# DVE's order at a tile's end: the rest of the transposed h ahead of the second norm's statistics, the normalising operation one lo part later

## The reference, cut to what matters

```python
# N = 4096 nodes, F = 256 features, 16 experts, hidden 512
h   = layernorm(x)
Wh  = h @ W; src = Wh @ a[:F]; dst = Wh @ a[F:]
att = softmax(where(adj > 0, leaky_relu(src + dst.T, 0.2), -9e15), axis=1)   # 4096 x 4096
h_prime = att @ Wh
gi = h_prime @ w_ih.T + b_ih; gh = h @ w_hh.T + b_hh          # 3F columns each
r = sigmoid(i_r + h_r); z = sigmoid(i_z + h_z); n = tanh(i_n + r * h_n)
x  = x + (1 - z) * n + z * h
xn2 = layernorm(x)                                           # the second norm
probs = softmax(xn2 @ gate_w + gate_b); top-2, renormalised
x  = x + sum over the two experts of weight * ((silu(xn2 @ w1) * (xn2 @ w2)) @ w3)
```

## Time and profile before

| | before |
|---|---|
| runs | 1268.34, 1272.80, 1272.82 us |
| median of the runs | 1272.8 us |
| profiled execution: its own time | 1271.41 us |
| its span | 1269.7 us |
| PE busy | 1158.3 us (91%) |
| PEld busy | 1052.3 us (83%) |
| DVE busy | 1044.5 us (82%) |
| ACT busy | 777.3 us (61%) |
| POOL busy | 354.0 us (28%) |

### The profile page before, as it was taken

One profiled execution on the slowest core, in us unless ns is written; L12 is line 12 of the kernel. 1 busy time (PEld: TensorE's weight loads), 2 busy tenths in 40 slices (PEclk: granted clock), 3 DMA queues, 4 the chain that ended last, 5 costly groups with the idle time before them and its releaser, 6 DMA issues.

```text
span 1269.7 us, 25947 instructions
## 1 busy us (share of the span) xinstructions
PE 1158.3 (91%) x7574; PEld 1052.3 (83%) x7575; DVE 1044.5 (82%) x2485; ACT 777.3 (61%) x1125; POOL 354.0 (28%) x351
## 2 busy tenths in 40 slices
PE   5979999999999999999999995379999999999995
PEld 4658989898989999998989894268888888888884
DVE  7957888888989898988888875978888888888883
ACT  3476767667676767676767641036666666666662
POOL 2521111111111111101011100036555555665554
PEclk9779999999999999999999998569999999999998
DMA  8232434343424343433333300232444455435430
GB/s 240 35 58 37 73 60 79 59 80 59 80 59 79 61 72 62 71 64 69 66 69 70 60 22 26 79 105 47 101 96 100 99 140 144 115 78 148 91 50 6
DMA packets 61633, 98.64 MB, mean 78 GB/s; under 512 B 9472, under 2 KB 36096, under 8 KB 61536
## 3 DMA queue, kind: packets, MB, share of 16 engines
q0 software_dynamic: 33600, 52.49, 25.9%
q1 hardware_dynamic: 27936, 44.93, 10.9%
HBM read 213.18 MB, written 18.81 MB: 183 GB/s over the span
## 4 chain that ended last, share of the span: by engine, by line
PE 73%; DVE 18%; issue 3%; ACT 2%; POOL 2%; DMA 1%; DVEq 0%; POOLq 0%
PE bank L1341 17%; PE bank L1092 13%; PE bank L1355 11%; PE bank L1218 8%; PE bank L1193 6%; PE bank L1192 6%; PE bank L1194 6%; PE bank L1223 4%; DVE pc L767 3%; DVE hT L793 2%; ACT pc L488 2%; POOL rs L440 1%; DVE xnv L722 1%; DVE scr L819 1%; DVE scr L820 1%
## 5 line engine op out<-in xcount | busy, mean ns | idle before, releaser
L1192 PE MATMUL bank<-V,pc 128*128 128x258 f32 x1024 | 310.7, 303 | 5.1 <-DVE pc L767 5.1
L1193 PE MATMUL bank<-V,pc 128*128 128x258 f32 x1024 | 290.9, 284 | 0.0
L1194 PE MATMUL bank<-V,pc 128*128 128x258 f32 x1024 | 288.6, 282 | 0.0
L1341 PE MATMUL bank<-wup,xT 128*128 128x512 f32 x948 | 240.3, 402 | 0.9 <-DVE xT L1039 0.9
L488 ACT ACTIVATE pc<-bank 128x512 fp32r<-128x512 f32 x256 | 152.2, 595 | 126.2 <-PE bank L1092 124.7
L767 DVE TENSOR_TENSOR pc<-bank,pc 128x512 fp32r<-128x512 f32 x256 | 175.7, 686 | 57.4 <-ACT pc L488 54.6
L1341 PEld LDWEIGHTS bank<-wup,xT 128*128 128x128 f32 x948 | 174.6, 191 | 35.6 <-DVE xT L1039 1.3
L1192 PEld LDWEIGHTS bank<-V,pc 128*128 128x128 f32 x1024 | 193.5, 189 | 6.2 <-DVE pc L767 6.2
L1193 PEld LDWEIGHTS bank<-V,pc 128*128 128x128 f32 x1024 | 195.5, 191 | 0.0
L1194 PEld LDWEIGHTS bank<-V,pc 128*128 128x128 f32 x1024 | 195.4, 191 | 0.0
L1034 DVE TENSOR_TENSOR wup<-wexp,wup 128x1024 fp32r<-128x1024 f32 x158 | 185.9, 1218 | 2.2 <-ACT wup L488 1.1
(11 more groups left out here) (159 smaller groups left out, 1573.9 us busy)
## 6 DMA issues: line engine op xcount, KB each, us to landing
wexp<-in_L_ffn_w SPq DMA_DIRECT2D x237, 512.0 KB
adjb<-in_adj POOLq DMA_DIRECT2D x128, 256.0 KB, 4.8
token_rows<-xrow SPq DMA_DIRECT2D x32, 130.0 KB, 2.1
E<-in_x SPq DMA_DIRECT2D x8, 512.0 KB, 9.0
xin<-in_x SPq DMA_DIRECT2D x32, 128.0 KB, 2.6
out<-xin SPq DMA_DIRECT2D x32, 128.0 KB, 1.7
xg<-token_rows,gidx POOLq DMA_INDIRECT x79
out<-ysc,cidx POOLq DMA_INDIRECT x79
```

The costliest lines, as they stand in the source:

```text
L1192: mm(acc[:, 0:VW], hi, V[:, j, 0, :], start=j == 0, stop=False)
L1193: mm(acc[:, 0:VW], hi, V[:, j, 1, :], start=False, stop=False)
L1194: ins = mm(acc[:, 0:VW], lo, V[:, j, 0, :], start=False, stop=j == T - 1)
L1341: ins = mm(acc[:, 0:HID], xT[:, r % WR, a, k * P:(k + 1) * P], wup[:, r % 2, n, b, k * HID:(k + 1) * HID], start=(k, a, b) == terms[0], st ...
```

## The change

`norm2` is cut into two functions: `norm2_statistics` holds bn_stats, bn_aggr and the variance, `norm2` holds the wait for POOL and the normalising operation. In step 6 `hT_lo` now comes first, behind the lo part, and the statistics behind it; the normalising operation follows in step 7, behind that step's lo part. In the written-out iteration 31 the statistics stay where they were and the normalising operation is put behind the last lo part. In the iterations after it nothing changes its place. No instruction is added or removed.

```diff
-            def norm2(i):
-                u = i % 2
+            def norm2_statistics(i):
                 dve.wait_ge(s_x1, i - 1)
                 link(V_.bn_stats(bst[:, 0, :], x1))
                 link(V_.bn_aggr(mv[:, :], bst[:, 0, :]))
                 V_.tensor_scalar(var[:, :], mv[:, 1:2], EPS, None, ALU.add).then_inc(s_var2, 1)
+
+            def norm2(i):
+                u = i % 2
                 dve.wait_ge(s_rs2, i - 1)
...
-                    if c == 6 and live(i, 2):
-                        norm2(i)
                     if c == 6 and live(i, 1):
                         hT_lo(i)
+                    if c == 6 and live(i, 2):
+                        norm2_statistics(i)
+                    if c == 7 and live(i, 2):
+                        norm2(i)
...
             chunk_lo(last + 6)
+            norm2_statistics(T - 1)
+            chunk_lo(last + 7)
             norm2(T - 1)
-            chunk_lo(last + 7)
...
+            norm2_statistics(T)
             norm2(T)
...
+            norm2_statistics(T + 1)
             norm2(T + 1)
```

## The result

The changed kernel takes 1241.17 us (median of 6 runs, 1235.03 to 1243.35) against 1272.04 us (6 runs, 1267.72 to 1272.82): ratio 0.9755, 95% interval 0.9724 to 0.9785. In a second set of runs it took 1241.66 us (5 runs) against 1269.75 us, ratio 0.9783 (0.9761 to 0.9805). The forecast was 1242.4 us.

The account below looks back on a forecast made before the run. PE was taken to bound the tile, interrupted once by its wait for hT_lo. Removing 35.4 us of waits, less 4.95 us for a DVE-ACT ring, gave -30.4 us: 1242.4 us median, range 1236 to 1251 at 8 in 10.

Parts of the forecast that it names:

- PE waits for hT_lo, worth 1.22 us a tile by distances: Before the GRU matmuls: moving hT_lo ahead of the statistics removes PE's wait in 29 tiles, 35.4 us.
- DVE gains 0.60 us by standing the lo part in POOL's time: At the tile's end: step 7's lo part runs during POOL's power, gaining DVE 0.60 us per tile.
- third rival: POOL's power is held up by the lo part or runs 1.04 us: ring 21.01 us, run 1257.0 us; chance 0.07.
- A ring of 20.51 us takes over after three or four tiles: From nmu through ACT's exponentials and hi parts, DVE's lo parts, to next nmu: 0.20 us above PE's 20.31.
- PE's wait would show as 4 to 5 us in total: In the profile after, PE's wait for hT_lo falls from 28.0 us to some 4 to 5 us.
- second rival: Longer ring, for example by x's reload or the n tanh: intervals 20.7 to 20.8 us, run 1249.8 us; chance 0.12.
- The clock stays: Over the 29 tiles PE's clock stays at 1.00; rival of a lower grant, 1303 us at 0.90, chance 0.02.
- The sum: PE's waits -35.4 us and the ring's +4.95 us make -30.4 us: profiled execution 1241.0 us, median 1242.4 us.
- term for the ring: Over 28 loop intervals the ring costs 0.20 us each, less the 0.65 us reserve before hT_lo: +4.95 us.

Follow-up runs that it names:

- two reliefs: Changed kernel with DVE's combine and remake_xn moved behind row_max, or ACT's fourth exponential moved behind the hi part of chunk 7: 1233.13 and 1234.42 us.
- two pads: Changed kernel plus one unused bn_stats per tile on DVE, behind remake_xn or behind route_weights in step 4: 1252.87 and 1241.46 us.
- part one alone: Kernel before with hT_lo first in step 6 and the whole norm behind it, ahead of step 7's lo part: 1255.97 us, ratio 0.9873.
- part two alone: Changed kernel with the statistics back ahead of hT_lo in step 6, normalising operation still behind step 7's lo part: 1239.98 us, ratio 0.9750.
- pad inside the ring: Changed kernel plus one unused bn_stats per tile on DVE behind remake_xn, ahead of the masks: 1252.87 us, ratio 0.9849.
- combine late: Changed kernel with combine and remake_xn moved from ahead of the masks to step 1, behind row_max: 1233.13 us, ratio 0.9704; again 1233.98 us.
- fourth exponential later: Changed kernel with ACT's fourth exponential moved from step 4 to step 5, behind the hi part of chunk 7: 1234.42 us, ratio 0.9693.
- swapped end: Kernel with combine late, plus iteration 32's GRU ahead of the transposes of xrow and the gate a chunk later: 1234.46 us, ratio 0.9708.
- pad outside: Changed kernel plus one unused bn_stats per tile on DVE in step 4, behind route_weights: 1241.46 us, ratio 0.9764.
- old order with combine late: Kernel before, old order at the tile's end kept, with combine and remake_xn moved to step 1: 1271.98 us, ratio 1.0007.

## Why the prediction was right, step by step

- *PE waits for hT_lo, worth 1.22 us a tile by distances.* Right: PE's own interval is 20.31 us, shown by 28 intervals in two kernels. The idle figure of the view of waits (0.96 us) would have given 20.57.
- *DVE gains 0.60 us by standing the lo part in POOL's time.* Right: the normalising operation starts 0.84 us behind the variance with the lo part inside, the recorded wait for POOL is gone (0.68 us before; 0.17 are left by distances, 0.16 were forecast), and POOL's power takes 0.56 us beside the lo part as it did beside an idle DVE. The third rival (power held up) falls. So the rule of the Trainium skill ("SBUF — State Buffer", section "Who interferes with whom"), by which a DVE instruction with at most one SBUF input, outside the two-port modes, doesn't contend with GpSimd, agrees with this trace: POOL's power has a median of 560 ns over 32 times, 561 ns before.
- *A ring of 20.51 us takes over after three or four tiles.* Right in place and size: 20.49 us, from the fifth interval of the loop on. The two reliefs, the two pads and part one alone bear out its members on both engines. What the prediction lacks is a sum for the other ring, the one by way of PE that sets the 20.45 us of part two alone. It did no harm here: with hT_lo 464.81 - 462.98 = 1.83 us earlier, it comes to an estimated 21.53 - 1.83 = 19.7 us in the changed kernel.
- *PE's wait would show as 4 to 5 us in total.* Wrong in what the view shows: it has 0.6 us, and only for the weight loads. The delay is there in the intervals (0.18 us each), yet it is shorter than the modelled overlap of two matmuls, and so is not counted as idle.
- *The slow reload of x as the second rival.* It happened, in single tiles: one interval of 20.91 us (20.98 from first GRU matmul to first GRU matmul, as the others here) and one of 20.65 in the first profile of the changed kernel, one of 20.98 in the second. At the first of them SP's issue of the row store took 1.48 us instead of its median 0.43, the reload behind it went out late, and DVE waited. The timelines of SP and DVE:

```profile
281.86 1.48 SPq L357 DMA_DIRECT2D token_rows<-xrow  x1
283.39 0.43 SPq L351 DMA_DIRECT2D xin<-in_x  x1
```

```profile
286.15 0.41 DVE L799 TENSOR_SCALAR xnb<-xin,xmv,rstd 128x256 f32<-128x256 f32 x1 [0.40 <-DMA xin<-in_x]
```

  Part two alone has two such intervals (20.61 and 20.52 us) and the pad inside the ring two (21.46 and 21.64), each behind an issue of 1.4 to 1.8 us on SP; why an issue takes so long is open. One or two intervals in 28, longer by 0.1 to 0.7 us, are no shift to the second rival's 20.75. In the kernel with combine late, remake_xn comes 8 us later and no such interval occurs in either of its profiles.
- *The clock stays.* Right: 1.00 over the stretch with PE busy without a break.
- *The sum.* 1241.0 us for the profiled execution was 6 us too high for this one, which had a short last stage; against the medians, 1242.4 and 1241.2 us. Its term for the ring, 4.95 us, met 4.96 (573.64 - 28 x 20.31) partly by luck: some 0.6 us of these are the two late reloads, which the sum doesn't have, and the ring alone was a little shorter than forecast. That the medians agree to 1.2 us is luck too, since the two sets of runs put the gain at 30.9 and 28.1 us (forecast 30.4).

## What to carry to other kernels

When one engine waits once per round for another, price the wait by the distance between starts against a passage that lacks it, and then add up the next-longest ring through the order of all engines before you book the whole gain: here it was 0.2 us behind and took back 5 of 35 us. Look for a second ring of nearly the same length as well. An engine with idle time can still be in the ring that binds; what counts is on which side of its wait an operation stands, and the same 0.42 us operation cost 0.47 us on one side and 0.08 on the other. A round trip to another engine can be covered by work that has to be done anyway and is not yet late: here a lo part of 0.60 us in that place brought 0.60 us a tile (21.09 to 20.49), and hT_lo ahead of the statistics or behind them then made no difference that the runs could tell.

## What the runs showed of the hardware that I had not expected

The last stage, which is the same code in all these kernels, took 428.3 us in the changed kernel's first profiled execution and 435.1 us in its second (from the first gather to the end), 428.3 and 434.8 us in the two of combine late, 432.9 us in the kernel before. Part of it lies behind the last matmul: 9.2 and 13.5 us in the two of the changed kernel, 9.1 and 13.5 in those of combine late, 13.5 before. The other part, 2.2 to 2.7 us, lies in the matmuls' own stretch. In the second profiles of both kernels the chain of work runs there through the indirect stores of outputs, of which each waits for the one before to land and takes mostly 3 to 5 us and at times 6 to 8.5, as in the chain of the kernel with the fourth exponential later:

```profile
1096.20 3.09 DMA out<-ysc,cidx
1100.22 4.40 DMA out<-ysc,cidx
1105.50 8.48 DMA out<-ysc,cidx
```

For the two kernels that have two profiles the last stage is most of the difference between them (6.8 of 8.2 us and 6.6 of 7.7). The runs of one kernel lie 3 to 13 us apart, and so the intervals, which repeat to 0.02 us but for the late reloads, settled the questions here that the medians could not.

The GRU product of iteration 33, after PE had been idle for most of 4 us (busy for 1.44 of them), ran at the lower of the two clocks, 1.2 GHz, in the changed kernel (granted 0.50 over its first 3 us, 4.46 us for its twelve wide matmuls) and at the full 2.4 GHz in the kernels with combine late and with the exponential later (1.00, 3.07 us). The stretch ahead looks alike in all of these. It does not go with the edits' gain: the grant there was 0.50 to 0.64 in seven of the twelve profiles (before, both of the changed kernel, both parts alone, the pad inside, the swapped end) and 1.00 in the other five (both of combine late, the exponential later, the pad outside, the old order with combine late). That is the 1.4 us behind the loop. The 2.7 us ahead of it go with a difference of the same kind: from 40 to 80 us, still in the first stage, the grant was 0.66 in the second profile of the changed kernel and 0.74 in that of combine late. What decides either was not tried.
